# Row scatters of the expert stage: gated by TensorE's later steps, and without an address check

## The reference

```python
x = _layernorm(x + attention(x))                  # 4096 tokens x 128
rw = _route(x, gate_w, gate_bias)                 # 8 of 64 experts for each token, with weights
expert_out = vmap(mlp)(Wg, Wu, Wd)                # mlp: silu(x @ gw.T) * (x @ uw.T) @ dw.T, 88 wide
out = einsum('eth,te->th', expert_out, rw) + shared_mlp(x)
x = _layernorm(x + out)
```

## Time and profile before

| | |
|---|---|
| median of 3 runs | 868.43 us (867.42 to 872.18) |
| profiled execution, span | 868.7 us |
| mean granted PE clock | 0.881 |
| PE busy | 698.5 us (80%) |
| DVE busy | 489.8 us (56%) |
| POOL busy | 548.9 us (63%), of it 256.9 in L444 and 266.4 in L463 |
| ACT busy | 322.0 us (37%) |

### The profile page before, as it was taken

One profiled execution on the slowest core, in us unless ns is written; L12 is line 12 of the kernel. 1 busy time (PEld: TensorE's weight loads), 2 busy tenths in 40 slices (PEclk: granted clock), 3 DMA queues, 4 the chain that ended last, 5 costly groups with the idle time before them and its releaser, 6 DMA issues.

```text
span 868.7 us, 17014 instructions
## 1 busy us (share of the span) xinstructions
PE 698.5 (80%) x4968; PEld 606.5 (70%) x4968; DVE 489.8 (56%) x1679; ACT 322.0 (37%) x867; POOL 548.9 (63%) x558
## 2 busy tenths in 40 slices
PE   5689797979888786767799998999897888961395
PEld 3567676767676666644587898988797887960385
DVE  2437878787777777755756663444334433430275
ACT  2224233333424242313043564664545536420032
POOL 0000277777777777676777777777777777777241
PEclk9898989897979796959579998999989989895599
DMA  8202041414141413111354444444434434311695
GB/s 199 77 1 89 15 140 59 144 62 142 59 142 60 137 52 107 51 61 47 98 149 123 118 122 126 117 108 130 115 102 127 110 100 115 104 41 51 263 408 215
DMA packets 89949, 97.47 MB, mean 112 GB/s; under 512 B 21836, under 2 KB 73780, under 8 KB 89859
## 3 DMA queue, kind: packets, MB, share of 16 engines
q1 hardware_dynamic: 67043, 58.45, 23.5%
q0 software_dynamic: 20992, 36.74, 12.5%
q10 hardware_dynamic: 1824, 1.19, 0.5%
HBM read 55.02 MB, written 42.34 MB: 112 GB/s over the span
## 4 chain that ended last, share of the span: by engine, by line
PE 38%; DVE 22%; issue 15%; POOL 12%; DMA 7%; SPq 2%; ACT 2%; POOLq 0%; ACTq 0%; DVEq 0%
POOL y_dram L463 12%; DMA y_dram<-arena 4%; PE fa L1215 3%; PE fc L1140 3%; PE pb L1165 3%; PE pa L1165 2%; PE fb L1140 2%; PE ba L1145 2%; DMA arena<-y_dram 2%; DVE arena L720 2%; PE fa L1145 2%; PE bb L1140 1%; PE bb L1361 1%; PE ba L1361 1%; PE fb L1382 1%
## 5 line engine op out<-in xcount | busy, mean ns | idle before, releaser
L463 POOL DMA_INDIRECT y_dram<-arena x272 | 266.4, 979 | 83.4 <-issue 73.8
L444 POOL DMA_INDIRECT rows_dram<-rows x256 | 256.9, 1004 | 97.6 <-issue 76.4
L435 POOL TENSOR_TENSOR rstd<-var_eps,minus_half 128x2 f32<-128x2 f32 (+1 forms) x24 | 25.3, 1055 | 132.6 <-DVE var_eps L662 132.6
L618 ACT ACTIVATE arena<-weights 128x176 f32 x384 | 99.0, 337 | 13.8 <-DVE arena L1025 13.2
L1079 DVE TENSOR_TENSOR arena<-bb,arena 128x512 f32<-128x512 f32 x34 | 23.5, 691 | 75.5 <-DMA y_dram<-arena 70.9
L1140 PE MATMUL fb<-arena 128*128 128x128 f32 x384 | 53.7, 284 | 14.6 <-DVE arena L720 14.0
L1140 PEld LDWEIGHTS fb<-arena 128*128 128x128 f32 x384 | 48.8, 195 | 20.9 <-DVE arena L720 13.5
L1079 DVE TENSOR_TENSOR arena<-ba,arena 128x512 f32<-128x512 f32 x34 | 23.5, 690 | 67.1 <-DMA y_dram<-arena 63.3
L1140 PEld LDWEIGHTS fc<-arena 128*128 128x128 f32 x384 | 50.0, 197 | 15.2 <-ACT arena L522 7.7
L607 ACT ACTIVATE arena<-fb 88x512 f32<-88x512 f32 x39 | 23.1, 592 | 99.3 <-PE fc L1382 89.2
L1361 PE MATMUL bb<-weights,arena 88*128 x336 | 47.9, 293 | 14.4 <-DVE arena L1113 13.8
(11 more groups left out here) (295 smaller groups left out, 1472.6 us busy)
## 6 DMA issues: line engine op xcount, KB each, us to landing
arena<-y_dram SPq DMA_DIRECT2D x16, 1024.0 KB, 12.1
arena<-rows_dram SPq DMA_DIRECT2D x192, 76.0 KB
weights<-experts SPq DMA_DIRECT2D x16, 608.0 KB
arena<-rows_dram SPq DMA_DIRECT2D x128, 38.0 KB
y_dram<-arena POOLq DMA_INDIRECT x272
rows_dram<-rows POOLq DMA_INDIRECT x256, 2.3
xc<-x_chan SPq DMA_DIRECT2D x8, 256.0 KB, 3.9
x_res<-x_tok SPq DMA_DIRECT2D x8, 256.0 KB, 3.0
```

The lines of the kernel that those rows point to most:

```text
L435: pool.tensor_tensor(rstd[b % 2][:, 0:tiles], var_eps[b % 2][:, 0:tiles], minus_half[:, 0:tiles], ALU.pow).then_inc(S.rstd_done, 1)
L444: pool.indirect_dma_start(rows_dram, bass.IndirectOffsetOnAxis(ap=slot_of(a)[:, i, k:k + 1], axis=0), rows[:, NT * a + i, :], None).then_i ...
L463: pool.indirect_dma_start(y_dram, bass.IndirectOffsetOnAxis(ap=go_to[:, t:t + 1], axis=0), y_sb[q % YRING][:, i, :], None, bounds_check=B ...
L618: ins = act.activation(w_here[n % 2][:, (parts(q) * i + h) * 2 * I:(parts(q) * i + h + 1) * 2 * I], weights[:, bass.ds(at[i], 2 * I)], ACT ...
```

## The change

Three of the four scatters of a quad get a wait on a semaphore of PE. With m the quad's step, the second scatter waits for gate and up of step m+2, the third for the turn of step m+4, and the fourth for the down product of step m+1 (each cut off at the last step). The scatters no longer check addresses. Instead, `y_dram` begins with 2048 spare rows (`SINK`), and an empty row is sent to one of them: DVE takes the larger of the row's place (0 for an empty row, at least 2048 for others) and a constant row number.

```diff
-NOWHERE = 1 << 20
+RING, YRING, W_RING = 4, 4, 6
+SINK = 4 * YRING * P
...
-K_ALL = K_CHUNK + 4
+K_SINK = K_CHUNK + 4
+K_ALL = K_SINK + 4 * YRING
...
-        y_dram = nc.dram_tensor("y_dram", [B * L * PLACES, D], F32, kind="Internal").ap()
+        y_dram = nc.dram_tensor("y_dram", [SINK + B * L * PLACES, D], F32, kind="Internal").ap()
...
                 pool.wait_ge(S.go_done, q + 1)
                 pool.wait_ge(S.ye_done, STEP_OF[q] + 1)
                 for i in range(4):
-                    t = 4 * q + i
+                    t, m = 4 * q + i, STEP_OF[q]
+                    if i == 1:
+                        pool.wait_ge(S.gu_mm, min(m + 3, LAST))
+                    if i == 2:
+                        pool.wait_ge(S.xt_mm, turns(min(m + 4, LAST - 1)))
+                    if i == 3:
+                        pool.wait_ge(S.ye_mm, min(m + 2, LAST))
                     pool.indirect_dma_start(y_dram, bass.IndirectOffsetOnAxis(ap=go_to[:, t:t + 1], axis=0),
-                                            y_sb[q % YRING][:, i, :], None, bounds_check=B * L * PLACES - 1,
-                                            oob_is_err=False).then_inc(ys[q % YRING], 16)
+                                            y_sb[q % YRING][:, i, :], None).then_inc(ys[q % YRING], 16)
...
-                    dve.tensor_scalar(go_to[:, 4 * q:4 * q + 4], w_at[q % W_RING][:, :, 1], float(NOWHERE), None, ALU.add).then_inc(S.go_done, 1)
+                    dve.tensor_tensor(go_to[:, 4 * q:4 * q + 4], w_at[q % W_RING][:, :, 1],
+                                      const[:, K_SINK + 4 * (q % YRING):K_SINK + 4 * (q % YRING) + 4], ALU.max).then_inc(S.go_done, 1)
...
+    consts[:, K_SINK:] = np.arange(4 * YRING)[None, :] * P + t[:, None]
```

More of the change, by code:

```diff
@@ L172, in block_program @@
         taken[0] = 0
-        RING, YRING, W_RING = 4, 4, 6
         x1s, act_s = [part(512) for _ in range(2)], part(1024)
@@ L416, in load_result @@
                 n = 2 * P * PLACES
-                sp.dma_start(y4[u % YIN], y_dram[u * n:(u + 1) * n, :].rearrange("(i p j) c -> p i j c", p=P, j=PLACES)
+                sp.dma_start(y4[u % YIN], y_dram[SINK + u * n:SINK + (u + 1) * n, :].rearrange("(i p j) c -> p i j c", p=P, j=PLACES)
                              ).then_inc(y4_in[u % YIN], 16)
@@ L1460 @@
     token = np.arange(B * NT)[None, :, None] * P + t[:, None, None]
-    places = (token * PLACES + np.arange(TOPK)[None, None, :] % PLACES - NOWHERE).astype(np.float32)
+    places = (token * PLACES + np.arange(TOPK)[None, None, :] % PLACES + SINK).astype(np.float32)
     arrays = {
```

## The result

| | before | changed |
|---|---|---|
| median | 869.32 us (867.42 to 872.18, 6 runs) | 863.84 us (861.46 to 866.78, 6 runs) |
| ratio | | 0.9941, 95% interval 0.9917 to 0.9965 |
| profiled execution, span | 868.7 us | 865.0 us (its own time 866.78 us) |
| mean granted PE clock | 0.881 | 0.875 |

A forecast was written before the change was run, and what follows sets the result against it. From about 501 us POOL's back-to-back scatters, 1.2841 us apart, were taken to bound the kernel. Only the check's removal counted: 868.43 - 4.8 = 863.6 us, waits, sink rows and DVE 0; range 861.8 to 869.0 us.

The forecast's parts named there:

- The address check: Scatters behind quad 8's release: dropping the check saves 20 ns on each of 239 intervals, 4.8 us; forecast's chance 0.55.
- the check costs nothing by itself: Rival: the 19 ns between the scatter medians belong to the tensors; 0 to 17 ns saved, 864.4 to 868.4 us; chance 0.27.
- it costs far more: Rival: shorter rows hide part of the check's cost; at 40 ns 9.6 us saved, 858.9 us; chance 0.08.
- The waits: Three new waits on PE before each quad's second to fourth scatters: met before POOL comes, cost 0; gates rival's chance 0.07.
- no PE line as releaser beyond a microsecond in all: Sign in the scatters' idle time: names only "issue" or DVE, with PE names totalling no more than a microsecond.
- My bound of 0.54 us for a wait: Gates rival: 0.84 against 0.30 us at quad 8 bounds each of 204 waits, 110 us in all; chance 0.07.
- The margin at quad 17: Quad 17's fourth scatter: starts 5.5 us after its down product ended; gain gathered until then only 0.8 us.
- Quad 8: Its first scatter, released by DVE, still starts near 501.3 us, after about 1.5 us idle; the first 32 scatters' 0.64 us is lost.
- the check's MOVE: 29 ns on POOL's sequencer ahead of each scatter: the sequencer is far ahead, so removing it brings nothing.
- up to it, PE sets the pace: Expert stage before quad 8's first scatter: PE sets the time; behind it, POOL does.
- DVE's instruction and the sink rows: New DVE form, 0 to 0.06 us more a quad, and 2,048 spare-row writes, 1 MB in 300 us: price 0 each.
- contention between POOL and a DVE instruction with two inputs in SBUF: Rival: DVE's new instruction shuts POOL out 0.17 us, 68 times, 11.6 us, giving 875.2 us; chance 0.03.

The follow-up runs named there:

- the run repeated: The changed kernel run once more as a control, nothing altered, beside the kernel before: 865.26 us, ratio 0.9948.

## Why the prediction was right

**The bound.** The stage is a closed row of scatters from quad 8 on, and the end follows its last start by a fixed time. In all ten traces it is 60.4 to 60.7 us from that start to the end of the span. But the row is less free of PE than the prediction had it. In the changed kernel's trace DVE ended quad 18's product at 551.39 and the scatter started at 552.56, which leaves 0.42 us beyond the 0.75 us of a release. By my estimate from this, scatters quicker by another 10 ns or so (0.42 us over the 40 from quad 8 to quad 18) would have begun to wait there in an execution like this one.

**The address check.** Forecast 20 ns an interval, from the middle between two readings of L444; 1.2841 less 1.2655 is 18.6 ns in the two profiles shown, and 21 ns is the difference of medians in a series on one chip. The range of 17 to 24 ns held. Part of the difference is the execution: the first profiled one of the changed kernel was a little slower for every scatter; its unchanged row scatters have a median of 963 ns, those of the kernel before 960. In the run repeated, where they have 960 too, the row took 301.83 us, 1.2629 each. The sum of 4.8 us stands against 4.4 us in the first trace, 5.1 us in the repeated one and 5.1 us by the ratio. That the median of 863.84 us lies only 0.2 us from the forecast 863.6 is luck in part: over six runs the kernel before had 869.32 us and not the 868.43 us that I started from, and the medians lie 5.5 us apart. (The low end of the range was reckoned with 239 x 0.028 = 6.6 us; it is 6.7 us, and nothing hangs on it.) That the check costs nothing by itself is refuted by the kernel with the check put back, and that it costs far more by the same numbers. The Trainium skill's page "DMA: Bandwidth & Descriptors", section "Anatomy of one DMA", calls descriptor generation small beside a DMA's roughly 2 us. The traces do not agree for these DMAs: a row scatter holds POOL for 0.96 us of the 2.3 us until it lands, and in a row of scatters on the path even 21 ns of it counted.

**The waits.** Forecast 0. Taking them away and adding them alone both left the time where it was. One sign that the prediction named for it was drawn too sharply: "no PE line as releaser beyond a microsecond in all". PE names stand at 15 gaps with 4.5 us in all, but each is the 0.3 us of a scatter that waits for nothing; the longest gap under a name is the sign to read, not the total. My bound of 0.54 us for a wait was a price of being released late, never of the instruction. Moving them by one step showed that the margin is real and how thin it is.

**The margin at quad 17.** Here one number of the working was off, without harm. I gave 5.5 us of room at the fourth scatter of quad 17, less 0.8 us of gain. In the changed kernel's trace PE's down product ended at 550.27 + 0.39 = 550.66 and the scatter started at 551.29: 0.63 us. The 5.5 us were those of one execution. (It is quad 18's down product that this scatter waits for, the same that quad 18's own first scatter hangs on.) PE's clock was 1.00 from 540 to 560 us there and 0.68 from 540 to 550 us in the changed one, where eight matmuls of the up product took 1.84 us in place of 1.04, and almost all of the room went, most of it on PE's side.

**Quad 8.** The idle time before its first scatter was forecast at about 1.5 us and was 1.34. With a check it is 0.78 to 0.87 us, without one 1.34 to 1.39 us, in seven traces: the quicker scatters ahead of it are given back there, as forecast. One small term was missed. The prediction gave the check's MOVE no price, since POOL's sequencer is far ahead of the engine. At quad 8 it is not: from DVE's end to the start of the scatter it is 0.83 us in the three traces with a check and 0.75 to 0.76 us in the four without, so 0.07 to 0.08 us came once in a run. In the other three it is 0.30 us: later waits had held POOL up at quad 6, the order of steps was moved, or PE was early by itself. In an execution of the last kind the row of scatters counts from its first start, and the gain of the first 32 is kept. So "up to it, PE sets the pace" is not true of every execution. The prediction called itself wrong if PE ran at its lower clock somewhere from 440 to 500 us. It did, and much alike in both traces: the granted clock was 0.84 before and 0.80 in the changed kernel from 440 to 450 us, and 1.00 from 450 to 500 us. The working survives this, since it only moves the moment at which quad 8 is ready, here by 0.73 us, and not the row behind it.

**DVE's instruction and the sink rows.** Forecast 0. The new instruction takes less time than the old one:

```profile
L1108 DVE TENSOR_TENSOR arena<-arena,const x68: 161/162/206, 439.0 to 767.6; 128x4 uint32<-128x4 f32 x68
```

The Trainium skill's page "GPSIMD Engine Reference", section "Key points", names contention between POOL and a DVE instruction with two inputs in SBUF. For these scatters the traces do not bear it out: in the changed kernel the 58 scatters beside which the new instruction ran took 962 ns in the mean and the other 214 took 961 ns, none is longer than 998 ns, and with the check put back the median is 979 ns as before.

## What to carry to other kernels

Where an engine issues small DMAs back to back and others wait for it, a few ns of each are worth looking for: compare the medians of two lines that differ in an option, and multiply by the intervals on the path. Making room for stray rows so that no address has to be checked is such an option, and it can be had without any waits. A wait that is met before the engine comes to it is free, but read its margin from several executions, since it can shrink from 5.5 us to 0.6 us with the clock of the engine that it waits for. And once the bound is made quicker, look for the place where the next engine is closest behind: here 0.3 to 0.5 us at quad 18, in three of the traces without a check.

## What the hardware showed

From the recorded end of DVE's instruction to the start of the scatter that it released took 0.75 us in the changed kernel (501.18 to 501.93) and 0.83 us before. From PE's recorded end it took 0.27 to 0.28 us in the kernel with later waits (492.09 to 492.37, 504.41 to 504.68). I had used 0.83 and 0.66 us for PE as well, which made its waits look nearer than they were. The two differ in more than the engine. The first scatter of a quad waits for two semaphores, and POOL's sequencer runs an instruction of its own for one of them, which is in the trace at 501.21, 0.72 us before the scatter; the second to fourth have one wait and no such instruction. PE's ends are modelled besides. Which of these makes the difference, no run tells.

The check's price was not the same on two lines: 20 to 21 ns on rows of 512 bytes and 11 to 14 ns on rows of 608 bytes. No run tells why; without a check both take about the same, 958 and 960 ns at the median.
